# A selective scan shared between VectorE and GpSimd: 15 of 48 products on GpSimd instead of 16

## The reference

```
dA_t = exp(delta_t * A[d, n])
h_t  = dA_t * h_(t-1) + (delta_t * u_t) * B_t[n]
y_t  = sum over n of h_t[d, n] * C_t[n]
```

## Time and profile before

| | us |
|---|---|
| median of 3 runs | 28432.66 |
| lowest and highest run | 28402.5, 28460.19 |
| span of the profiled execution | 28422.8 |
| its busy time: PE, DVE, ACT, POOL | 23013.8, 25435.4, 14594.8, 22836.6 |
| mean granted clock of PE, share of full | 0.839 |

### The profile page before, as it was taken

How to read it: one execution, slowest core, us unless ns; L and a number is a source line. 1 busy time by engine, 2 the same in 40 slices (tenths; PEclk the granted TensorE clock), 3 DMA queues, 4 the chain that set the end, 5 groups by cost and what they waited for, 6 DMA issues and landing times. The chain is left out here.

```text
span 28422.8 us, 328026 instructions
## 1 busy us (share of the span) xinstructions
PE 23013.8 (81%) x97488; PEld 6745.8 (24%) x97488; DVE 25435.4 (89%) x16259; ACT 14594.8 (51%) x20067; POOL 22836.6 (80%) x10240
## 2 busy tenths in 40 slices
PE   8888888888576888888887888888875888888885
PEld 3322222222232222222233222222212322222222
DVE  3489999999579999999986999999997899999997
ACT  1255555555266555555514655555552655555552
POOL 0169999999036999999981799999990499999992
PEclk9978888888766888888868888888887888888887
DMA  2242222121454222212266422122226622222224
GB/s 86 97 138 45 49 49 49 40 48 41 157 187 160 49 49 49 47 41 49 49 218 218 130 49 49 42 46 49 49 58 216 203 48 49 49 45 43 49 49 146
DMA packets 1121174, 2332.84 MB, mean 82 GB/s; under 512 B 98406, under 2 KB 609347, under 8 KB 1110717
## 3 DMA queue, kind: packets, MB, share of 16 engines
q1 hardware_dynamic: 1117572, 2308.66, 29.8%
q10 hardware_dynamic: 1728, 1.70, 0.0%
HBM read 1329.40 MB, written 980.58 MB: 81 GB/s over the span
## 5 line engine op out<-in xcount | busy, mean ns | idle before, releaser
L1589 POOL TENSOR_TENSOR scan_hc<-scan_bc,scan_h 128x1024 f32<-128x1024 f32 x6912 | 16065.4, 2354 | 116.6 <-DVE scan_h L1766 115.7
L1766 DVE TENSOR_TENSOR_SCAN scan_h<-scan_da,scan_state,scan_dbu 128x1024 f32<-128x1024 f32 x6912 | 15989.1, 2338 | 141.4 <-ACT scan_da L1643 135.4
L1680 PE MATMUL scan_da<-scan_dd,scan_ssel 32*128 32x512 f32 x27648 | 9115.9, 746 | 3002.1 <-DVE scan_h L1766 2768.0
L1643 ACT ACTIVATE scan_da<-scan_da,scan_a_cur 128x1024 f32<-128x1024 f32 x6912 | 7516.2, 1087 | 7740.0 <-PE scan_da L1680 7734.7
L1680 PE MATMUL scan_p_du<-scan_dd,scan_ssel 32*128 32x512 f32 x27648 | 9207.7, 745 | 449.2 <-DVE scan_dbu L1753 170.8
L1753 DVE TENSOR_TENSOR scan_dbu<-scan_p_du,scan_bc 128x1024 f32<-128x1024 f32 x4608 | 5561.5, 1207 | 375.3 <-PE scan_p_du L1680 336.6
L1575 POOL TENSOR_TENSOR scan_dbu<-scan_bc,scan_dus 128x1024 f32<-128x1024 f32 x2304 | 5427.2, 2356 | 58.6 <-ACT scan_dus L1617 57.5
L1680 PEld LDWEIGHTS scan_da<-scan_dd,scan_ssel 32*128 32x128 f32 x27648 | 2456.7, 217 | 10300.7 <-DVE scan_h L1766 8724.7
L1697 PE MATMUL scan_p_y<-scan_hc,scan_rsel 128*32 128x512 f32 x27648 | 4781.9, 773 | 20.7 <-POOL scan_hc L1589 20.6
L1680 PEld LDWEIGHTS scan_p_du<-scan_dd,scan_ssel 32*128 32x128 f32 x27648 | 2416.3, 212 | 3522.1 <-DVE scan_dbu L1753 2947.5
L1622 ACT ACTIVATE scan_state<-scan_h,scan_a_cur 128x1 f32<-128x1 f32 x6912 | 2023.5, 293 | 1575.4 <-DVE scan_h L1766 1465.2
(11 more groups left out here) (225 smaller groups left out, 13400.7 us busy)
## 6 DMA issues: line engine op xcount, KB each, us to landing
scan_bc<-bc_d SPq DMA_DIRECT2D x576, 512.0 KB, 12.0
du_d<-prep_useq SPq DMA_DIRECT2D x384, 576.0 KB, 3.7
delta_d<-prep_delta SPq DMA_DIRECT2D x384, 576.0 KB, 4.6
y_d<-scan_y SPq DMA_DIRECT2D x576, 384.0 KB, 5.2
scan_dd<-delta_d SPq DMA_DIRECT2D x1136, 192.0 KB, 4.8
scan_dd<-du_d SPq DMA_DIRECT2D x1136, 192.0 KB, 6.5
fin_y<-y_d SPq DMA_DIRECT2D x288, 576.0 KB, 5.6
xs_d<-proj_xs_o SPq DMA_DIRECT2D x96, 588.0 KB, 3.3
```

The lines of the kernel that those rows point to most:

```text
L1589: nc.gpsimd.tensor_tensor(hc[:, u % HC_SLOTS, :], c, h[:, u % H_SLOTS, :], ALU.mult).then_inc(hc_ready, 1)
L1643: nc.scalar.activation(da[u % DELTA_BANKS][:], da[u % DELTA_BANKS][:], ACT.Exp, scale=a_cur[:, slot(u)[0], u % UNITS:u % UNITS + 1]).then_ ...
L1680: return nc.tensor.matmul(dst[:, half * H:(half + 1) * H], ssel[rows, i, :], dd[rows, s, m, j, :], start=True, stop=True)
L1766: nc.vector.tensor_tensor_scan(h[:, v % H_SLOTS, :], da[v % DELTA_BANKS][:], dbu[:, v % DBU_SLOTS, :], state[:, v % UNITS:v % UNITS + 1], ...
```

## The change

In each 48 units, 15 are shared instead of 16. They stand at 2, 5, 8, 11 and 15 of each 16, so that the distances are 3, 3, 3, 4 and again 3. POOL makes 15 products with B in a chunk, DVE 33, ACT makes 15 copies. Counts and distances that were worked out from TRIO now come from helper functions. PE's and ACT's look ahead goes to the next shared unit, three or four ahead; POOL issues the product with B for the shared unit behind the coming one, at the unit before that one.

```diff
-TRIO = 3
+SHARED = tuple(b + u for b in range(0, UNITS, 16) for u in (2, 5, 8, 11, 15))
+SHARES = UNROLL * len(SHARED)
+PRODUCTS = ROUND - SHARES
...
 def shared(u):
-    return u % TRIO == 2
+    return u % UNITS in SHARED
+
+def shares(u):
+    return sum(shared(v) for v in range(u))
+
+def products(u):
+    return u - shares(u)
+
+def next_share(u):
+    return next(v for v in range(u + 1, u + UNITS) if shared(v))
...
 # POOL
                 def share(r, u):
-                    g.wait_ge(share_copied, r * (ROUND // TRIO) + (u // TRIO + 1) + ONE)
+                    g.wait_ge(share_copied, r * SHARES + (shares(u) + 1) + ONE)
...
-                        ahead = u + TRIO + 1
-                        if shared(ahead) and not (last and ahead >= ROUND):
-                            share(r, ahead)
+                        if shared(u + 1):
+                            ahead = next_share(u + 1)
+                            if not (last and ahead >= ROUND):
+                                share(r, ahead)
...
 # ACT
-                        if shared(u) and not (last and u + TRIO >= ROUND):
-                            copy_share(r, u + TRIO)
+                        if shared(u) and not (last and next_share(u) >= ROUND):
+                            copy_share(r, next_share(u))
...
 # PE
-                        t.wait_ge(dbu_ready, r * (ROUND // TRIO * 2) + (u // TRIO * 2 + u % TRIO) + ONE)
+                        t.wait_ge(dbu_ready, r * PRODUCTS + products(u) + ONE)
                         if not shared(u):
-                            t.wait_ge(share_copied, r * (ROUND // TRIO) + (u // TRIO + 1) + ONE)
+                            t.wait_ge(share_copied, r * SHARES + (shares(u) + 1) + ONE)
                             spread(p_du, 1, u, 0)
                             spread(p_du, 1, u, 1).then_inc(du_spread, 1)
-                        elif not (last and u + TRIO >= ROUND):
-                            spread_share(r, u + TRIO)
+                        elif not (last and next_share(u) >= ROUND):
+                            spread_share(r, next_share(u))
```

More of the change, by code:

```diff
@@ L1575, in share @@
                     nc.gpsimd.tensor_tensor(dbu[:, u % DBU_SLOTS, :], bc[:, s, image(u % UNITS), :],
-                                            dus[:, u // TRIO % DUS_SLOTS, :], ALU.mult).then_inc(share_ready, 1)
+                                            dus[:, shares(u) % DUS_SLOTS, :], ALU.mult).then_inc(share_ready, 1)
                 def rounds(r, last):
@@ L1594, in _ @@
                 g.memset(state[:], 0.0).then_inc(zeroed, 1)
-                for u in range(TRIO):
-                    if shared(u):
-                        share(0, u)
+                share(0, SHARED[0])
                 rounds(0, False)
@@ L1613, in copy_share @@
                 def copy_share(r, u):
-                    a.wait_ge(share_spread, r * (ROUND // TRIO) + (u // TRIO + 1) + ONE)
-                    a.wait_ge(share_ready, nth(r * (ROUND // TRIO), u // TRIO - DUS_SLOTS + 1) + ONE)
-                    nc.scalar.activation(dus[:, u // TRIO % DUS_SLOTS, :], p_du[:], ACT.Copy).then_inc(share_copied, 1)
+                    a.wait_ge(share_spread, r * SHARES + (shares(u) + 1) + ONE)
+                    a.wait_ge(share_ready, nth(r * SHARES, shares(u) - DUS_SLOTS + 1) + ONE)
+                    nc.scalar.activation(dus[:, shares(u) % DUS_SLOTS, :], p_du[:], ACT.Copy).then_inc(share_copied, 1)
                 def keep(r, u):
@@ L1662, in _ @@
                 a.wait_ge(zeroed, 1 + ONE)
-                for u in range(TRIO):
-                    if shared(u):
-                        copy_share(0, u)
+                copy_share(0, SHARED[0])
                 rounds(0, True, False)
@@ L1705, in rounds @@
                         if u % UNITS == UNITS - 1 and not (last and u == ROUND - 1):
-                            s, n = slot(u + TRIO)
+                            s, n = slot(next_share(u))
                             t.wait_ge(loaded[s], r * (TURNS * LOADS) + n * LOADS + ONE)
-                        if first and u == FIRST_UNITS - TRIO:
+                        if first and u == SHARED[1]:
                             t.wait_ge(loaded[0], LOADS + ONE)
-                        t.wait_ge(dbu_ready, r * (ROUND // TRIO * 2) + (u // TRIO * 2 + u % TRIO) + ONE)
+                        t.wait_ge(dbu_ready, r * PRODUCTS + products(u) + ONE)
                         if not shared(u):
-                            t.wait_ge(share_copied, r * (ROUND // TRIO) + (u // TRIO + 1) + ONE)
+                            t.wait_ge(share_copied, r * SHARES + (shares(u) + 1) + ONE)
                             spread(p_du, 1, u, 0)
                             spread(p_du, 1, u, 1).then_inc(du_spread, 1)
-                        elif not (last and u + TRIO >= ROUND):
-                            spread_share(r, u + TRIO)
+                        elif not (last and next_share(u) >= ROUND):
+                            spread_share(r, next_share(u))
                         if u % PAIR == 1 and (u >= SUM_LAG or not first):
@@ L1730, in _ @@
                 t.wait_ge(first_loaded, FIRST_LOADS + ONE)
-                for u in range(TRIO):
-                    if shared(u):
-                        spread_share(0, u)
+                spread_share(0, SHARED[0])
                 rounds(0, True, False)
@@ L1749, in times_b @@
                         d.wait_ge(loaded[s], r * (TURNS * LOADS) + n * LOADS + ONE)
-                    d.wait_ge(du_spread, r * (ROUND // TRIO * 2) + (u // TRIO * 2 + u % TRIO + 1) + ONE)
+                    d.wait_ge(du_spread, r * PRODUCTS + (products(u) + 1) + ONE)
                     d.wait_ge(scanned, nth(r * ROUND, u - DBU_SLOTS + 1) + ONE)
@@ L1759, in recur @@
                     if shared(u):
-                        d.wait_ge(share_ready, r * (ROUND // TRIO) + (u // TRIO + 1) + ONE)
+                        d.wait_ge(share_ready, r * SHARES + (shares(u) + 1) + ONE)
                     else:
-                        d.wait_ge(dbu_ready, r * (ROUND // TRIO * 2) + (u // TRIO * 2 + u % TRIO + 1) + ONE)
+                        d.wait_ge(dbu_ready, r * PRODUCTS + (products(u) + 1) + ONE)
                     d.wait_ge(kept, nth(r * ROUND, u - H_SLOTS + 1) + ONE)
```

## The result

The changed kernel takes 29528.42 us (median of 4 runs, 29465.84 to 29548.22) against 28431.03 us before: a ratio of 1.0381, 95% interval [1.0368, 1.0394]. It is slower, as forecast, but by 1097 us instead of 104, and far outside the range.

The account below looks back on a forecast made before the run. DVE, plus stalls from PE and ACT, was taken to bound the kernel. 1.11 - 0.20 - 0.15 = 0.76 us in each of 144 chunks, +109 us, less 6 us of phase ends, gave 28536 us; 8 in 10 range 28450 to 28610.

Parts of the forecast that it names:

- DVE's path, POOL's work at nothing: Scan phases: DVE plus stalls from PE and ACT set the pace; POOL's saving of 2.31 us a chunk counts nothing.
- (a): DVE in the scans: 33 products a chunk instead of 32, on the path, +1.11 us a chunk, upper bound 1.21.
- (c): One p_du hand-over through PE and ACT fewer a chunk: -0.20 us of 3.2 us stalls, bounds 0 and -0.40.
- (d): PE's low clock, 0.26 of scan time, partly hides DVE's extra product: -0.15 us a chunk, bounds nothing and -0.29.
- more low clock: Rival: PE's clock in the scans falls more often, stalls grow 0.64 us a chunk, 92 us on top, 28628; chance 0.07.
- POOL decides: Rival: POOL paces the scans, so each chunk falls by 2.31 us, 333 us in all, to 28100; chance 0.08.

Follow-up runs that it names:

- The run with the product twice: Kernel before the change, but DVE makes one ordinary product with B of each chunk (unit 22) twice, first into a spare buffer: 28895.02 us, ratio 1.0166.

## Why the prediction was wrong

- *DVE's path, POOL's work at nothing.* Right: the run with POOL's old load gives the changed kernel's time, and DVE is not among those who waited for POOL's products with C in the changed kernel.
- *(a), +1.11 us a chunk.* The duration was right, the effect was not. The run with the product twice shows 3.3 us a chunk in the pattern of before: the step leaves out what the added time does to PE, whose wait at that place it took from 0.73 to 1.64 us.
- *(c), one hand-over fewer, -0.20 us, bounds 0 and -0.40.* This is the step that failed. It took the 3.2 us of stalls as a price that every hand-over has alike, and scaled them by 15/16. Measured, the stalls grew by 6.9 us a chunk (993 us over 144). A hand-over costs nothing at the high clock and 1.5 to 1.6 us at the low one with the sums in it, and the change brought those two together: 432 x 1.50 = 648 us behind unit 15 of each 16 alone. A chunk takes 5629/36 = 156.4 us with its back edges, where 147.5 to 148 without them was forecast. The text said that no row separated odd from even units and put that into bounds, and it named this as the way in which it could be wrong above all; I could have separated them with the starts in the trace. The rows were also read wrongly: the 0.46 us wait that was put to a hand-over stood behind PE's sums of an ordinary unit.
- *(d), low clock takes 0.26 of the time.* It was taken as a constant, and the extra product as partly hidden there, -0.15 us. The clock is an outcome: 0.78 to 0.98 in the scans of these kernels, by where PE has gaps. And nothing was hidden: the product made twice cost three times its own length.
- *The rival "more low clock".* Its sign, a clock under 0.85 in the scans, came: 0.81. It had the clock right and left out the place, and so had the wrong size. It scaled the old stalls with the low clock's share, 92 us on top, where stalls had gone from 695 to 1688 us while that share went from 0.27 to 0.38. It was argued down by PE's busy share, which hardly moves; what decides is how PE's work is bunched. The Trainium skill, TensorE: Matmul & The Clock Gate, section Part 1: The HAM clock gate, says that the low rate is what PE falls back to and that activity releases it. The trace agrees: two more matmuls at a unit took the scans from 0.81 to 0.96. I had read the earlier trace rows against it, a low stretch in which PE is busy throughout; but at 1.2 GHz the same work looks twice as long (the sums 1.94 us for 1.07), so a busy low stretch says nothing of why the clock had fallen.
- *POOL decides.* Wrong for the kernel as it was, right once the clock holds: 190 us faster instead of the 333 in the rival, since DVE's own 144.8 us (143.7 and the 1.11 of the product) and 294 us of stalls, the back edges among them, come next.

That the time still came out slower, as forecast, is no proof of the sum: of the 7.9 us that a chunk grew (1141 over 144) the sum had 0.76.

What stays open: the runs show that PE's gaps bring the low clock and that it keeps to a place in the pattern, not why it settles on the place that it does, nor that it could be foretold for a new pattern.

## What to carry to other kernels

Where PE's clock falls with its own gaps, as here, a change of rhythm on another engine can cost many times its instructions: look up in the trace at which units the low clock falls, and what is in the chain there, before scaling stalls by a count. If PE sits in short waits, matmuls that change nothing, small enough to fit into the wait, can buy more than they cost; measure two sizes, since a third matmul at each place cost 1300 us here. And test a change of balance between engines with the clock held: here the same change is 3.8% slower without and 0.7% faster with it.

## What was not expected of the hardware

The scans with 23288 matmuls each were faster than those with 20716: adding them took 1361 us, 4.6%, off the changed kernel. Mean clock and time did not go together: 28653 us at 0.855 against 29035 us at 0.848, and 29468 us at 0.928 against 28167 us at 0.915.
